# A mixture-of-experts and gated-scan kernel: the third tile group's router behind the first expert segment

## What is computed

```python
x = x + 0.5 * ffn(layernorm(x), Wr, br, W1, b1, W2, b2)
x = x + attn(layernorm(x), gamma, wq, wk, wv, wa, wg, wo)
x = x + 0.5 * ffn(layernorm(x), Wr, br, W1, b1, W2, b2)

# ffn: 16 experts, each token goes to its two best
probs = softmax(xt @ Wr + br);  w, idx = top_k(probs, 2);  w = w / sum(w)
h = gelu(einsum('td,edh->teh', xt, W1) + b1)      # 128 -> 256
o = einsum('teh,eho->teo', h, W2) + b2            # 256 -> 128
y = xt + einsum('teo,te->to', o, comb)            # comb holds w at idx

# attn: a gated linear recurrence over the 256 tokens of a sequence
q, k, v, a, g = xn @ (wq, wk, wv, wa, wg)         # xn: RMS norm
a = sigmoid(|a|) * exp(i * angle(a));  y_t = a_t * y_(t-1) + k_t * v_t
out = (q * real(y) * silu(g)) @ wo
```

## Time and profile before

| | |
|---|---|
| median of 3 runs | 871.86 us (868.15 to 876.06) |
| the profiled execution | 871.79 us, its span 870.1 us |
| instructions in the profile | 15790 |
| share of the span busy | PE 80%, POOL 70%, PEld 66%, DVE 62%, ACT 59% |
| mean TensorE clock granted | 0.867 of full speed |
| HBM traffic | 191 GB/s over the span |

### The profile page before, as it was taken

How to read it: one execution, slowest core, us unless ns; L and a number is a source line. 1 busy time by engine, 2 the same in 40 slices (tenths; PEclk the granted TensorE clock), 3 DMA queues, 4 the chain that set the end, 5 groups by cost and what they waited for, 6 DMA issues and landing times.

```text
span 870.1 us, 15790 instructions
## 1 busy us (share of the span) xinstructions
PE 695.0 (80%) x4409; PEld 576.3 (66%) x4410; DVE 540.1 (62%) x1281; ACT 512.9 (59%) x1064; POOL 612.7 (70%) x551
## 2 busy tenths in 40 slices
PE   4667999998876998786878769896689779989880
PEld 4253988886366973486843769734669669879770
DVE  5897200318779996699964799875989648010311
ACT  1211567667778657777577676576676336646450
POOL 3377560677788887888877657778687778776575
PEclk9655799999968998888989689986798889999995
DMA  9897699894147661366733167541386657979882
GB/s 330 297 374 235 176 271 262 247 285 137 43 128 219 202 188 48 113 177 179 225 112 96 54 192 211 179 120 39 110 258 195 205 154 211 275 225 274 282 264 90
DMA packets 189278, 167.13 MB, mean 192 GB/s; under 512 B 19024, under 2 KB 176528, under 8 KB 188304
## 3 DMA queue, kind: packets, MB, share of 16 engines
q1 hardware_dynamic: 121168, 106.83, 40.6%
q0 software_dynamic: 16384, 33.72, 12.7%
q10 hardware_dynamic: 51648, 25.63, 10.0%
HBM read 104.57 MB, written 61.51 MB: 191 GB/s over the span
## 4 chain that ended last, share of the span: by engine, by line
PE 49%; ACT 15%; DVE 12%; DMA 11%; issue 5%; POOL 4%; SPq 2%; ACTq 0%; POOLq 0%; DVEq 0%
PE bank L793 16%; PE bank L810 14%; PE bank L870 8%; DMA WUP<-up_weights 7%; PE bank L719 4%; PE bank L783 4%; ACT eo L546 2%; PE bank L709 2%; DMA rows_out<-eo 2%; POOL rows_in L472 2%; DVE stats L922 1%; PE bank L882 1%; POOL rows_in L480 1%; ACT XT L588 1%; ACT kv L508 1%
## 5 line engine op out<-in xcount | busy, mean ns | idle before, releaser
L493 POOL DMA_INDIRECT got<-rows_out,IDX x256 | 290.9, 1136 | 119.8 <-issue 71.5
L793 PE MATMUL bank<-xsT,WUP 128*128 128x128 f32 x1564 | 230.0, 294 | 47.0 <-ACT xsT L557 34.1
L793 PEld LDWEIGHTS bank<-xsT,WUP 128*128 128x128 f32 x1564 | 208.5, 207 | 56.1 <-issue 39.5
L472 POOL DMA_INDIRECT rows_in<-XL,IDX x128 | 167.1, 1305 | 83.8 <-issue 33.9
L810 PE MATMUL bank<-W,hidT 128*128 x1564 | 214.8, 281 | 3.9 <-issue 1.6
L810 PEld LDWEIGHTS bank<-W,hidT 128*128 128x128 f32 x1564 | 193.8, 195 | 10.6 <-issue 7.1
L480 POOL DMA_INDIRECT rows_in<-XL,IDX x128 | 141.4, 1105 | 44.3 <-issue 27.8
L538 ACT ACTIVATE hidT<-bank 128x512 f32<-128x512 f32 x200 | 117.5, 588 | 86.6 <-PE bank L793 86.3
L546 ACT ACTIVATE eo<-bank,xs 128x128 f32<-128x128 f32 x391 | 122.2, 363 | 70.3 <-PE bank L810 64.4
L870 PE MATMUL bank<-XT,WA 128*128 128x512 f32 x192 | 93.4, 646 | 17.1 <-DVE qg L1087 9.7
L557 ACT ACTIVATE xsT<-bank 128x256 f32<-128x256 f32 x200 | 73.5, 373 | 41.6 <-PE bank L783 40.1
(11 more groups left out here) (144 smaller groups left out, 843.3 us busy)
## 6 DMA issues: line engine op xcount, KB each, us to landing
WUP<-up_weights SPq DMA_DIRECT2D x400, 128.0 KB
xs<-rows_in SPq DMA_DIRECT2D x100, 258.0 KB, 4.5
rows_out<-eo ACTq DMA_DIRECT2D x91, 256.0 KB
rows_in<-kv SPq DMA_DIRECT2D x16, 774.0 KB, 12.1
rows_in<-XL,IDX POOLq DMA_INDIRECT x256, 3.5
got<-rows_out,IDX POOLq DMA_INDIRECT x256
out<-X SPq DMA_DIRECT2D x4, 1024.0 KB, 5.9
X<-in_L_attn_x SPq DMA_DIRECT2D x3, 1024.0 KB, 11.8
```

The costliest lines, as they stand in the source:

```text
L472: pool.indirect_dma_start(rows_in[slot], bass.IndirectOffsetOnAxis(IDX[:, g, j, 0:1], 0), XL[:, b, j, :], None).then_inc(first_put[i], 16)
L493: pool.indirect_dma_start(got[:, k, j, :], None, rows_out[SLOT[f, g, half]][0:rows, :], bass.IndirectOffsetOnAxis(IDX[:, g, j, k:k + 1], 0 ...
L793: ins = pe.matmul(ps[2 + u % 2][:, k * P:(k + 1) * P], WUP[:, u, a, c * P:(c + 1) * P], xsT[:, u % 2, a * P:(a + 1) * P], start=True, stop ...
```

## The change

One entry of the list, the router of the third group, moves behind the first expert segment and the entry of the gather that follows it. Nothing else is touched.

```diff
-         ("K", 0, 1, 0), ("L", 6, 8), ("W", 0, 1), ("B", 0, 0, 1), ("B0", 0, 1), ("R", 0, 2), ("E", 0, 0, 0, 0, 24),
-         ("G", 0, 1, 0, 4), ("Q", 0, 2), ("K", 0, 2, 0), ("C", 0, 0, 0, 4), ("P", 0, 3, 0), ("E", 0, 1, 0, 0, 24),
+         ("K", 0, 1, 0), ("L", 6, 8), ("W", 0, 1), ("B", 0, 0, 1), ("B0", 0, 1), ("E", 0, 0, 0, 0, 24),
+         ("G", 0, 1, 0, 4), ("R", 0, 2), ("Q", 0, 2), ("K", 0, 2, 0), ("C", 0, 0, 0, 4), ("P", 0, 3, 0), ("E", 0, 1, 0, 0, 24),
```

## The result

| | before | after |
|---|---|---|
| median | 870.86 us (20 runs) | 878.15 us (20 runs) |
| ratio, 95% interval | | 1.008 (1.0054 to 1.0105), that is +7.0 us (+4.7 to +9.1) |
| profiled execution, its span | 871.79, 870.1 us | 878.77, 877.0 us |
| mean granted clock | 0.867 | 0.894 |

The changed kernel is slower by 0.8%. The forecast of 881.2 us is 3 us high, and 878.15 lies in its range. As a difference, +9.4 us was forecast and +7.0 measured. (The ratio leaves out the runs in the slower state, while the medians hold all 20 and differ by 7.3 us.) The two profiled executions differ by 6.98 us, so the traces can be compared place by place.

A forecast was written before the change was run, and what follows sets the result against it. No engine was taken as full; the chain that ended last, 49% PE, ran through the edit. The terms -4.4 + 7.5 + 6.1 + 0.2 = +9.4 us on 871.8 gave 881.2 us, range 875.5 to 886.5.

The forecast's parts named there:

- the first rival: Part of the loss is absorbed by weight loads, clock and slack behind the router: +5.1 us, 877; chance 0.14.
- In front of the segment: First expert segment starts at 88.1 instead of 92.48, held by the landing of xs: -4.4 us.
- The clock at the segment's head: First segment's start: full clock after some 5 us, today about 6; half of that 1 us could return.
- The router behind the segment: After the first segment's last down product PE runs the router, sized from router (1,3): +7.5 us.
- The mask wait: PE's rank product L730 waits idle behind the router for DVE's mask, sized from group (1,1): +6.1 us.
- The head of the second segment: From L730 to the second segment's first down product, at half clock, 5.49 us against 5.25: +0.2 us.
- The sum: -4.4 + 7.5 + 6.1 + 0.2 = +9.4 us for the second segment and all behind it.
- Does it reach the end: Group 0's last gather moves by the same 9.4 us, tied to the second segment's pairs; nothing later absorbs it.
- The second, no change at all: PE's list of work is unchanged, so the whole kernel's time stays at 872 us; chance 0.04.
- The third, faster: First segment's earlier start outweighs the router behind it, 867.2 us with the full 10.2 gained; chance 0.02.
- The fourth: Dearer: router at half clock (10.2 us), first segment's start wins only 2 us: +15.8, 887.6 us; chance 0.08.
- same: Whole kernel's time within about 1%, 8.7 us, of the time before, border at 880.6 us; chance 0.47.

The follow-up runs named there:

- moved_again: The changed kernel itself, run again beside others on one chip; 1.0088 of the kernel before.
- gather_free: Changed kernel with group 0's gather counts set to at most 24, the end of the first segment; 1.0107 of the kernel before.
- split_only_again: Changed kernel with the second expert segment cut into 8 and 16 pairs, back to back; 1.0114 of the kernel before, 1.0065 on the slow chip.
- warm: Changed kernel with 24 unread products of the identity on PE ahead of the mask wait; 1.0111 of the kernel before.
- rank_later_again: Changed kernel with the second segment cut after 8 pairs and group 2's share, rank products, additions and scatter placed there; 1.0044 of the kernel before.
- twice_again: Changed kernel with unread router-like PE work (16 transposes, 16 products) ahead of the first segment; 1.0182 of the kernel before.
- early_turns_again: Kernel before with 12 of the 16 transposes of group 2's router issued earlier, ahead of L756; 0.9983 of the kernel before.
- early_both: Kernel before with 12 early router transposes and group 0's gather counts set to 24; 0.998 of the kernel before, 865.09 us.

## Why the prediction was right, step by step

Its order of events on PE was right up to the second segment, and the sum there too. The end, +7.0 us, lies 2.4 below the forecast's +9.4 and 1.9 above the first rival's +5.1. So the direction and the place of the loss were forecast by the right mechanism, and the size at the end was met only roughly, by a path behind the second segment that the forecast had in part wrong.

**In front of the segment: forecast -4.4, measured -3.8.** The mechanism held: the wait for xs sets the start. The start was 89.46, not 88.1. 0.8 of the 1.4 us lie ahead of the edit: L756 starts at 82.65 where it started at 81.87, and SP issued xs at 84.71, not 83.88. The rest is the landing, 4.62 us, which was at most 4.3 before. Why it took longer stays open: from 84 to 88 the DMA share was 0.81, and 0.88 before. Counted from L756, the segment starts after 6.81 us where it was 10.61.

**The clock at the segment's head: left to the range, measured -0.75.** From L783 to the first L810 it is 4.88 us and was 5.63. The clock rose 5 us earlier, as the window of 93 to 98 shows. Against it, the segment from there to its end took 0.95 us more (94.34 to 145.35, before 98.11 to 148.17), so together they come to +0.2. The forecast had said that the weights should be no later limit; further into the segment they are: PE's waits for WUP from the first L810 to the segment's end come to 4.0 us in three waits, and to 0.7 us in one wait before. What the earlier clock gives is used up there.

**The router behind the segment: forecast 7.5, measured 6.5.** From 145.35 to DVE's bias add at 151.82 it is 6.47 us. This is the term mis-sized most. I took it from router (1,3), where the clock had fallen towards the end (the last eight products took 1.87 us); here it stayed at 1.00 in the window of 147 to 151, and the last eight took 1.06. The lower bound that I had worked out, 6.1 with the wait for ACT, was the nearer one. The wait for ACT was 0.75. How far the clock falls here is a matter of the single execution: from L709 to L990 it is 6.48 us in moved_again and 6.46 in gather_free, but 7.88 in split_only_again and 8.14 in warm, in which the same instructions stand. So 7.5 was a fair figure, and the meeting of the sum below is in part luck.

**The mask wait: forecast 6.1, measured 6.04** (151.82 to 157.86). DVE's operations between are those of group (1,1), and the analogue of the same order elsewhere in the same trace gave the price to 0.1 us.

**The head of the second segment: forecast +0.2, measured -0.24** (5.01 against 5.25). The clock was at half, as forecast, and the wait for xs and the table load for the share were covered; it came back sooner than at (1,1), where the same stretch took 5.49. The load is at the place the forecast named (timeline of ACT in the kernel after):

```profile
159.76 1.28 ACT L538 ACT_TABLE_LOAD   x1
161.54 0.60 ACT L538 ACTIVATE hidT<-bank 128x512 f32<-128x512 f32 x1 [0.50 <-PE bank L793]
```

The Gelu follows 0.50 us behind the load's end, and PE's product, not the table, released it. In the kernel before there is a closer case: the load of 1.28 us at 149.20 ends at 150.48, and the sigmoid stands 0.01 behind it.

```profile
150.49 0.22 ACT L522 ACTIVATE share<-gap 128x16 f32<-128x16 f32 x1
```

The extra drain of about 1.38 us that the Trainium skill (ScalarE: Activation LUTs, section "What ACT_TABLE_LOAD costs") puts on each switch isn't to be seen here either, and the sum without it was the right one.

**The sum: forecast +9.4; -3.8 - 0.75 + 0.95 + 6.47 + 6.04 - 0.24 = +8.7 by the edit, +9.45 with the 0.8 ahead of it.** So the sum for the place is met almost exactly, and by errors that cancel: the router is 1.0 us cheaper, the 0.8 ahead of the edit was in no term, and the start gains 0.6 less, beside smaller ones.

**Does it reach the end: here the argument failed in two steps.** First, the gathers. The forecast read from the chain that the 17th pair's output move at 193.96 releases the last gather at 194.67, and so gave the gathers no slack. Both readings were wrong. The moves of ACT and the gathers, in the kernel before:

```profile
188.86 0.62 ACT L546 ACTIVATE eo<-bank,xs 128x128 f32<-128x128 f32 x2 [0.47 <-PE bank L810]
190.95 0.62 ACT L546 ACTIVATE eo<-bank,xs 128x128 f32<-128x128 f32 x2 [0.15 <-PE bank L810]
192.17 0.94 POOL L493 DMA_INDIRECT got<-rows_out,IDX  x1 [0.30 <-issue]
194.67 0.94 POOL L493 DMA_INDIRECT got<-rows_out,IDX  x1 [0.31 <-ACT eo L546]
```

and in the kernel after:

```profile
198.83 0.62 ACT L546 ACTIVATE eo<-bank,xs 128x128 f32<-128x128 f32 x2 [0.24 <-PE bank L810]
199.72 0.94 POOL L493 DMA_INDIRECT got<-rows_out,IDX  x1 [0.41 <-ACT eo L546]
202.22 0.94 POOL L493 DMA_INDIRECT got<-rows_out,IDX  x1 [0.30 <-issue]
```

The moves come once for each pair; counted from 154.55, those at 188.86 and 190.95 are the 16th and the 17th, and the one at 193.96 is the 18th. So the last gather's pair was done 2.8 us before POOL came to it. POOL was at its own pace, one gather each 1.25 us, and its usual 0.30 us of idle was ascribed to a move that happened to end then. The gather at 192.17, the third from the end, waits for the 16th pair and had 2.4 us of slack. After the change that pair is 10.0 us later (198.83), the gather starts when it is done, at 199.72, and the slack is used up: +7.55 there and at the last gather. The last landing takes 0.8 us longer. Thus the last addition moved by 8.3 (198.35 to 206.67), not 9.4, and with it L844, where PE's idle shrank:

```profile
213.60 1.88 PE L765 MATMUL bank<-B,CT 128*128 128x512 f32 x4
215.89 0.66 PE L844 MATMUL bank<-ident,kv 128*128 128x128 f32 x4 [0.41 <-DVE kv L977]
```

PE came to L765 10.1 us later (213.60 against 203.52), L844 8.3 later, with 0.41 us of idle left of 2.17. So 1.8 us of PE's delay fell into idle time, of which the forecast had said that it would be used only if the gathers came free. gather_free shows the other side: with the gathers free the place is held by PE. After the change the two limits are 0.4 us apart.

Second, "nothing later hangs on anything that is not moved along". Two places behind did not move along, by the clock and by a transfer. At the first recurrence the granted clock fell, where it had been full before. In the kernel after:

```profile
222.70 0.41 PE L756 MATMUL bank<-ident,ranks 128*128 128x128 f32 x2 [2.46 <-DVE X L1059]
222.00:230.00 8.00, 7.30 (x15) 3.32 (x16) 7.41 (x39) 5.13 (x11) 5.80 (x8) 0.79 0.15 48
```

and the same place in the kernel before:

```profile
214.38 0.41 PE L756 MATMUL bank<-ident,ranks 128*128 128x128 f32 x2 [1.32 <-DVE X L1059]
222.00:230.00 8.00, 7.55 (x19) 3.14 (x18) 7.91 (x18) 5.61 (x9) 6.37 (x6) 1.00 0.13 41
```

The router (0,3) behind it came 11.8 us late instead of 8.3: 3.5 us more. PE had stood idle for 2.46 us ahead of this place and for 1.32 before. The traces of the second and third group of runs sort the same way, with one doubt. In moved_again, rank_later_again, twice_again, split_only_again and early_turns_again PE idles 2.22 to 2.46 us there, and the mean clock of the next two windows (2 and 4 us) is 0.60 to 0.80; in gather_free and early_both it idles 0.87 us, and the clock stays at 1.00. But it also stays at 1.00 in warm, behind 2.17 us. So longer idle and lower clock mostly go together, and the length of the idle alone is not shown to be what decides. The five kernels include early_turns_again, in which the router is not moved, so the 3.5 us are not shown to be part of the change's own mechanism. What the kernel before usually has there, one trace can't tell.

The third group's second expert segment gave 3.3 us back. In the kernel before:

```profile
689.42 1.09 PE L783 MATMUL bank<-ident,xs 128*128 128x128 f32 x4 [3.53 <-DMA xs<-rows_in]
690.00:694.00 4.00, 3.86 (x19) 3.49 (x18) 3.48 (x22) 1.64 (x4) 2.92 (x4) 0.50 0.48 149
```

and in the kernel after:

```profile
700.45 0.63 PE L783 MATMUL bank<-ident,xs 128*128 128x128 f32 x4 [1.45 <-DMA xs<-rows_in]
698.00:702.00 4.00, 2.20 (x18) 1.83 (x18) 3.62 (x14) 0.66 (x2) 3.06 (x4) 1.00 0.91 248
```

PE waits for xs 2.1 us less (1.45 against 3.53), and the head runs at full clock: 3.27 us to the first L810 (703.72) where it took 5.62 (695.04). The 2.35 us of the clock differ from trace to trace: in all eight traces of the second and third group of runs the first L783 here takes 0.63 or 0.74 us, so it is at or near the full level. But only in moved_again and gather_free does the head take 3.27 us; in the six others the clock falls within the head, and it takes 4.62 to 4.86 us, in early_turns_again and early_both too, where the router stands in its old place. So the trace of before has the dearest head of all and that of after one of the cheapest, and part of the 2.35 us is chance. Together the fall here and the rise at the recurrence cancel to within 0.3 us: the difference is 8.3 at L844 and 8.3 again at router (1,3). Another 1.4 us are given back between there and the end, in steps that I didn't follow.

**The rivals.** The first (+5.1, part absorbed) had its slack right: 1.8 us of 2.17 were used. Its other two parts came to nothing: PE's waits for WUP in the second segment are 2.4 us and were 2.8, those in the first rose by 3.3, and what the earlier clock brought went into these. The second, no change at all, has failed: the ratio's interval is above 1. It rested on the rule of the Trainium skill (Perfetto Trace Analysis, section "Identifying the Most-Contended Engine") to judge by the highest occupancy; that an edit of the order alone then does nothing was my inference. Here the busy time of PE even fell by 6.1 us while the time rose. The third, faster, did not occur. The fourth failed in its two premises: the router did not run at half clock, and the start won 3.8 us, not 2.

The change of 0.8% lies just within the 1% of "same" (0.47), and the interval reaches to 1.05%: it stands at the border at which the two chances had been split.

## What to carry to other kernels

A step that feeds another engine and gets its answer back on its own queue has a latency beside its work. If it is moved directly ahead of its first reader, the whole latency (here DVE's 6 us of masking) becomes idle time, though no engine has more work. A releaser in the chain is inferred: before giving a wait no slack, look whether the engine was idle there for longer than its usual gap. Read the price at a place of the same trace where the steps already stand in that order, and ask for the clock there too; it is the clock that made router (1,3) 1 us too dear as a model. Expect that part of a loss in one stage is gained or lost again at the next waits, and look at the idle of the stages behind before saying that all of it reaches the end.

## What the hardware showed

- The same program took 868 and 866 us on two chips and 1003 us on a third. In split_only on the third chip the products themselves take almost the same time (L793 300 ns on average, 292 in moved_again), but the output moves of ACT have 114.9 us of idle ahead of them, where moved_again on another chip has 72.0. The lines by group, first split_only, then moved_again:

```profile
L546 ACT ACTIVATE eo<-bank,xs 128x128 f32<-128x128 f32 x391 | 122.3, 367 | 114.9 <-PE bank L810 70.4 <-remote 29.2 <-issue 14.0
```

```profile
L546 ACT ACTIVATE eo<-bank,xs 128x128 f32<-128x128 f32 x391 | 122.5, 364 | 72.0 <-PE bank L810 59.4 <-DMA rows_out<-eo 10.8 <-issue 1.2
```

  What makes these waits longer there stays open. On that chip the mask wait is again 6.14 us, as it holds nothing but DVE's work.
- The granted clock fell to half within the router's last products while PE was busy without a break: eight L719 took 0.96, then 1.73, then 1.87 us in warm, at 147.56, 148.97 and 150.54; the clock was 0.92 from 147 to 149 and 0.50 from 149 to 151.
- It can stay at half with PE busy: in rank_later_again it is 0.50 from 153 to 157, with no idle in that stretch.
- A filler in a wait can cost more than it saves: 24 products of 128x128 took 8.43 us, at 0.50 for the first 5 us and 0.84 after.
